# Attention denominators packed and spread by transfers, the first maxima moved into the projection

## The reference

```python
# x: (4, 1024, 128); H = 16 heads of hd = 8
xn = layernorm(layernorm(x)) * ln_g + ln_b
q, k, v = split(xn @ w_qkv + b_qkv)                       # (4, 16, 1024, 8) each
scores = einsum('bhqd,bhkd->bhqk', q, k) * hd ** -0.5
bias = (rel_pe @ w_rel)[i - j + t - 1]                    # relative position, per head
out = einsum('bhqk,bhkd->bhqd', softmax(scores + bias), v) @ w_out + b_out
x = x + layernorm(out)
# 64 experts, 8 per token, picked within 4 of 8 groups, 128 slots per expert
weights = sigmoid(layernorm(x) @ gate.T) ...              # top-k with group limits
y = sum over the 8 experts of weight * (silu(x w1) * (x w3)) w2, plus a shared expert
x = x + layernorm(y)
```

## Time and profile before

| | us |
|---|---|
| median of 3 runs (1178.47 to 1181.9) | 1181.58 |
| profiled execution | 1185.66 |
| its span, first to last instruction | 1183.8 |
| PE busy (share of the span) | 888.7 (75%) |
| DVE busy | 808.8 (68%) |
| ACT busy | 692.4 (58%) |
| POOL busy | 591.1 (50%) |
| maxima, 512 slots on DVE (mean 1.217) | 600.0 |
| reciprocal of the denominators, 8 on DVE (mean 3.344) | 26.7 |

### The profile page before, as it was taken

One profiled execution on the slowest core, in us unless ns is written; L12 is line 12 of the kernel. 1 busy time (PEld: TensorE's weight loads), 2 busy tenths in 40 slices (PEclk: granted clock), 3 DMA queues, 4 the chain that ended last, 5 costly groups with the idle time before them and its releaser, 6 DMA issues. The chain is left out here.

```text
span 1183.8 us, 16193 instructions
## 1 busy us (share of the span) xinstructions
PE 888.7 (75%) x5090; PEld 285.7 (24%) x5090; DVE 808.8 (68%) x1223; ACT 692.4 (58%) x1433; POOL 591.1 (50%) x732
## 2 busy tenths in 40 slices
PE   4647999999899999999999999999964520555400
PEld 1311222222222222222222222222212310444300
DVE  7858988889789989988988987988612310111117
ACT  4723677777687777777778767776862210322204
POOL 4720010122456455545635734654575855588847
PEclk9866999999999999999999999999996675656555
DMA  3796211133311132220002220000000010767555
GB/s 99 211 241 113 61 52 35 45 84 90 83 36 34 36 71 58 60 41 8 7 7 42 64 45 7 8 11 6 8 11 11 28 38 4 192 134 136 88 112 192
DMA packets 115499, 77.18 MB, mean 65 GB/s; under 512 B 41503, under 2 KB 99355, under 8 KB 115414
## 3 DMA queue, kind: packets, MB, share of 16 engines
q1 hardware_dynamic: 91638, 66.63, 21.5%
q0 software_dynamic: 21504, 6.79, 4.9%
q10 hardware_dynamic: 2272, 2.73, 1.3%
HBM read 38.48 MB, written 54.69 MB: 79 GB/s over the span
## 5 line engine op out<-in xcount | busy, mean ns | idle before, releaser
L737 DVE TENSOR_REDUCE half_max<-s_pair 128x2 f32<-128x1024 f32 x512 | 600.0, 1217 | 89.9 <-PE s_pair L1257 81.6
L1194 ACT ACTIVATE probs<-st_bank 128x512 f32<-128x512 f32 x1024 | 543.9, 603 | 184.7 <-PE st_bank L1270 163.8
L1057 POOL DMA_INDIRECT table<-rows,keys_i x256 | 256.6, 1003 | 178.8 <-issue 71.6
L1270 PE MATMUL st_bank<-q_stack,k_stack 98*128 98x512 bf16 (+1 forms) x1024 | 326.0, 388 | 15.4 <-issue 8.4
L1279 PE MATMUL pv_bank<-probs,values 128*16 128x512 f32 x2048 | 274.9, 608 | 4.3 <-ACT unit_out L1128 4.2
L1257 PE MATMUL s_pair<-k_stack,q_stack 64*128 64x512 bf16 x1024 | 203.5, 397 | 29.3 <-DVE half_max L737 28.2
L1257 PEld LDWEIGHTS s_pair<-k_stack,q_stack 64*128 64x128 bf16 x1024 | 48.8, 93 | 342.0 <-issue 197.9
L1270 PEld LDWEIGHTS st_bank<-q_stack,k_stack 98*128 98x128 bf16 (+1 forms) x1024 | 78.9, 97 | 177.3 <-issue 95.8
L1456 POOL DMA_INDIRECT sums<-out,ids x64 | 99.7, 1558 | 41.5 <-ACT out L1511 20.3
L1470 DVE CAST ids<-xe 128x4 uint32<-128x4 f32 x16 | 2.8, 174 | 135.4 <-DMA sums<-out,ids 83.4
L952 POOL CAST shift<-minus_max 128x16 bf16<-128x16 f32 x32 | 6.5, 202 | 117.0 <-DVE minus_max L744 116.9
(11 more groups left out here) (181 smaller groups left out, 793.9 us busy)
## 6 DMA issues: line engine op xcount, KB each, us to landing
table<-blank SPq DMA_DIRECT2D x8, 772.0 KB, 4.7
xe<-table SPq DMA_DIRECT2D x16, 386.0 KB, 5.0
q_stack<-q_image SPq DMA_DIRECT2D x96, 64.0 KB
k_stack<-k_image SPq DMA_DIRECT2D x96, 64.0 KB
s<-sums SPq DMA_DIRECT2D x24, 256.0 KB, 6.5
k_image<-k_piece SPq DMA_DIRECT2D x16, 256.0 KB, 3.1
table<-rows,keys_i POOLq DMA_INDIRECT x256
sums<-zeros SPq DMA_DIRECT2D x16, 256.0 KB
```

What stands on the lines that cost most here:

```text
L737: V.tensor_reduce(half_max[n % 2][:, h:HG:SIDE_HEADS, tile, half], s_pair[slot % S_SLOTS][:].rearrange("p (s k) -> p s k", s=SIDES), AX.X, ...
L1057: pool.indirect_dma_start(out=table, out_offset=bass.IndirectOffsetOnAxis(ap=keys_i[c % 2][:, pick:pick + 1], axis=0), in_=rows[c % 2][:, ...
L1194: A.activation(probs[:, s % P_SLOTS, :], st_bank[at % ST_BANKS][:], ACT.Exp).then_inc(bank_free, 1)
L1270: M(bank(at)[:], k_stack[g][own, tile // PER, h, tile % PER * P:(tile % PER + 1) * P], q_stack[g][own, half, h, :], start=True, stop=True) ...
```

## The change

**Values and denominators.** A head's eight value columns are followed by one column of ones (`VW` = 9) instead of eight. They are made in the projection (`vst`, two memsets on POOL instead of one on DVE) and stored and loaded with the values, as one piece per partition. `move_out` now packs the denominator row of each head into eight partitions of 64 (`packed`, 128x64), four transfers, and moves the sums by four. DVE takes the reciprocal of `packed`, and SP spreads it to `recip_t` (128x512) by eight transfers (`spread_reciprocals`), which POOL's `normalise` waits for. In SP's order this stands behind the unit's load and ahead of `put_shift(n+1)`.

**First maxima.** The 16 slots of unit 0 move to the end of the projection's block, on PE and DVE. The pair banks of the projection (psT, psQ) are now the `s_pair` banks. SP's loads back are placed one chunk later. ACT issues the bias rows of groups 1 and 2 in the attention block, SP those of group 3 behind its loads.

**Places.** The lead of 26 is reached by one more slot in 16 steps instead of 8. Reciprocal at (0, 14) for (0, 18), normalise at (0, 6) for (0, 5), y at (0, 28) for (0, 26), and the steps behind it.

**Table clears.** Two in each of units 0 to 3 instead of one in each of units 0 to 7.

```diff
+VW = HD + 1
...
-    engine.dma_start(stacks.values[:, g, :, 0, :], v_columns[:, g, b * TILES_T:(b + 1) * TILES_T]).then_inc(stacks.loaded[g], 16)
+    engine.dma_start(stacks.values[:, g].rearrange("p k c -> p (k c)"), v_columns[:, g, b * TILES_T:(b + 1) * TILES_T].rearrange("p k c -> p (k c)")).then_inc(stacks.loaded[g], 16)
...
-                if c == 1:
+                elif c == 1:
                     sp.wait_ge(bias_stored, 16 * 6)
-                if c in (1, 2):
-                    load_bias_queries(sp, stacks, bias_q_image, 0, c - 1)
-                    load_bias_keys(sp, stacks, bias_k_image, c - 1)
-                if c == 3:
+                    for side in range(SIDES):
+                        load_bias_queries(sp, stacks, bias_q_image, 0, side)
+                elif c in (2, 3):
+                    load_bias_keys(sp, stacks, bias_k_image, c - 2)
+                elif c == 4:
                     for v in range(2):
                         sp.wait_ge(q_stored[v], 16)
                         sp.wait_ge(k_stored[v], 32)
                         sp.wait_ge(v_stored[v], 16)
-                if c in (3, 4):
-                    load_side(sp, stacks, q_image, k_image, 0, 0, c - 3)
-                if c == 5:
+                if c in (4, 5):
+                    load_side(sp, stacks, q_image, k_image, 0, 0, c - 4)
+                elif c == 6:
...
-            V.memset(stacks.values[:, :, :, 1, :].rearrange("p g k c -> p (g k) c"), 1.0).then_inc(stacks.gaps_done, 1)
...
+            for slot in range(SLOTS):
+                row_max(dve, nc, stacks, slot)
...
+            for a in range(2):
+                G.memset(vst[a][:].rearrange("p g j (h c) -> p (g j h) c", h=HG)[:, :, HD:VW], 1.0).then_inc(ones_made, 1)
...
+            pe.wait_ge(xnT_done, CHUNKS)
+            pe.wait_ge(q_full_done, CHUNKS)
+            for slot in range(SLOTS):
+                row_scores(pe, nc, stacks, slot)
...
-RING_AT = {"y": (0, 26), "xf": (1, 28), "logits": (1, 31), "ranks": (3, 4)}
-NORM_Y, NORM_XF = (1, 4), (1, 22)
-RECIP, STATS_Y, STATS_X1 = (0, 18), (0, 30), (1, 14)
+RING_AT = {"y": (0, 28), "xf": (1, 28), "logits": (1, 31), "ranks": (3, 4)}
+NORM_Y, NORM_XF = (1, 5), (1, 22)
+RECIP, STATS_Y, STATS_X1 = (0, 14), (1, 0), (1, 14)
...
-NORMALISE, OUT_NORM, RESIDUAL, RES_NORM = (0, 5), (0, 7), (1, 2), (1, 5)
+NORMALISE, OUT_NORM, RESIDUAL, RES_NORM = (0, 6), (1, 0), (1, 2), (1, 5)
...
-    return 22 if n == 0 else 18
+    return (22, 20)[n] if n < 2 else 18
...
-    return min(ALL_UNITS * SLOTS, step // 2 + 1 + FIRST_LEAD + min(LEAD - FIRST_LEAD, step // 8))
+    return min(ALL_UNITS * SLOTS, step // 2 + 1 + FIRST_LEAD + min(LEAD - FIRST_LEAD, step // 16))
...
-                for h in range(HG):
-                    to = slice((HG * g + h) * HD, (HG * g + h + 1) * HD)
-                    for v, dst in enumerate((sums_t, denominators)):
-                        sp.dma_start(dst[to, :], unit_out[PART * h + v * HD:PART * h + (v + 1) * HD, :]).then_inc(unit_moved, 16)
+                    sp.wait_ge(recip_moved, SPREAD * c)
+                heads = range(HG * g, HG * (g + 1))
+                for h in heads:
+                    sp.dma_start(packed[HD * h:HD * (h + 1), :], unit_out[PART * (h % HG) + HD:PART * (h % HG) + VW, :]).then_inc(unit_moved, 16)
+                for h in heads:
+                    sp.dma_start(sums_t[HD * h:HD * (h + 1), :], unit_out[PART * (h % HG):PART * (h % HG) + HD, :]).then_inc(unit_moved, 16)
+
+            def spread_reciprocals(c):
+
+                sp.wait_ge(recip_done, c + 1)
+                if c >= 1:
+                    sp.wait_ge(normed_done, c)
+                for d in range(HD):
+                    sp.dma_start(recip_t[d:P:HD, :], packed[:]).then_inc(recip_moved, 16)
 
             load(sp, 0, 1)
...
+            for side in range(SIDES):
+                load_bias_queries(sp, stacks, bias_q_image, GROUPS - 1, side)
+                copy_bias_keys(sp, stacks, GROUPS - 1, side)
...
+                if n >= GROUPS and g == 0:
+                    spread_reciprocals(routed(n))
...
-                if n < CHUNKS:
+                if n < CHUNKS // 2:
+
                     experts = E // CHUNKS
-                    sp.dma_start(table[n * experts * CAP:(n + 1) * experts * CAP, :].rearrange("(e p) d -> p e d", p=P),
-                                 blank[:].rearrange("p (o d) -> p o d", o=1).to_broadcast([P, experts, ROW])).then_inc(blanked, 16)
-                elif n < 2 * CHUNKS:
+                    for part in (2 * n, 2 * n + 1):
+                        sp.dma_start(table[part * experts * CAP:(part + 1) * experts * CAP, :].rearrange("(e p) d -> p e d", p=P),
+                                     blank[:].rearrange("p (o d) -> p o d", o=1).to_broadcast([P, experts, ROW])).then_inc(blanked, 16)
+                elif CHUNKS <= n < 2 * CHUNKS:
                     for s in sums[1:]:
                         sp.dma_start(s[(n - CHUNKS) * CHUNK:(n - CHUNKS + 1) * CHUNK, :].rearrange("(t p) d -> p t d", p=P),
...
+            spread_reciprocals(CHUNKS - 1)
...
-                V.reciprocal(denominators[:], denominators[:]).then_inc(recip_done, 1)
+                V.reciprocal(packed[:], packed[:]).then_inc(recip_done, 1)
...
-                pool.wait_ge(recip_done, c + 1)
+                pool.wait_ge(recip_moved, SPREAD * (c + 1))
+                pool.wait_ge(unit_moved, MOVED * GROUPS * (c + 1))
                 if c >= 1:
                     pool.wait_ge(bank_ready, after(place["y", c - 1]))
-                G.tensor_tensor(att[:], sums_t[:], denominators[:], ALU.mult).then_inc(normed_done, 1)
+                G.tensor_tensor(att[:], sums_t[:], recip_t[:], ALU.mult).then_inc(normed_done, 1)
...
-            for g in range(1, GROUPS):
+            for g in (1, 2):
...
-                    mm = M(pv_bank[PART * h:PART * h + 2 * HD, :],
-                           values[:, n % GROUPS, tile].rearrange("p u c -> p (u c)")[:, h:2 * HD * HG:HG],
+                    mm = M(pv_bank[PART * h:PART * h + VW, :], values[:, n % GROUPS, tile, VW * h:VW * (h + 1)],
                            probs[:, (s + h) % P_SLOTS, :], start=(tile == 0), stop=(tile == TILES_T - 1),
```

More of the change, by code:

```diff
@@ L166, with unit_of, row_scores, row_max @@
 LOAD_BIAS = (16 * 9 * SIDES,) + (16 * 5 * SIDES,) * (GROUPS - 1)
+def unit_of(n):
+    return n // UNITS, n % UNITS // GROUPS, n % GROUPS
+def row_scores(pe, nc, stacks, slot):
+    n, i = slot // SLOTS, slot % SLOTS
+    b, half, g = unit_of(n)
+    h, tile, keys = i // 8, i // 2 % PER, i % 2
+    if i == 0 and half == 0:
+        pe.wait_ge(stacks.loaded[g], (b + 1) * LOAD)
+        pe.wait_ge(stacks.bias_rows_in[g], LOAD_BIAS[g])
+    if slot >= S_SLOTS:
+        pe.wait_ge(stacks.max_done, slot - S_SLOTS + 1)
+    for side in range(SIDES):
+        own, head = slice(MAIN_AT[side], MAIN_AT[side] + HALF_ROWS), SIDE_HEADS * side + h
+        mm = nc.tensor.matmul(stacks.s_pair[slot % S_SLOTS][:, side * CHUNK:(side + 1) * CHUNK],
+                              stacks.q[g][own, half, head, tile * P:(tile + 1) * P],
+                              stacks.k[g][own, keys, head, :], start=True, stop=True)
+    mm.then_inc(stacks.s_ready, 1)
+def row_max(dve, nc, stacks, slot, shift_done=None):
+    n, i = slot // SLOTS, slot % SLOTS
+    h, tile, half = i // 8, i // 2 % PER, i % 2
+    halves = stacks.half_max[n % 2]
+    dve.wait_ge(stacks.s_ready, slot + 1)
+    nc.vector.tensor_reduce(halves[:, h:HG:SIDE_HEADS, tile, half], stacks.s_pair[slot % S_SLOTS][:].rearrange("p (s k) -> p s k", s=SIDES),
+                            AX.X, ALU.max).then_inc(stacks.max_done, 1)
+    if i == SLOTS - 1:
+        dve.wait_ge(stacks.max_done, (n + 1) * SLOTS)
+        if n >= 1:
+            dve.wait_ge(shift_done, SHIFT_ROWS * n)
+        nc.vector.tensor_reduce(stacks.minus_max[:], halves[:].rearrange("p h t k -> p (h t) k"),
+                                AX.X, ALU.max, negate=True).then_inc(stacks.row_max_done, 1)
 def project_tokens(nc, x, ln_g, ln_b, w_qkv, b_qkv, w_rel_rows, q_table, k_table, ident_in, ident,
@@ L1244, in bank @@
                 return st_bank[at % ST_BANKS]
-            def row_scores(slot):
-                n, i = slot // SLOTS, slot % SLOTS
-                b, half, g = unit_of(n)
-                h, tile, keys_ = i // 8, i // 2 % PER, i % 2
-                if i == 0 and half == 0:
-                    pe.wait_ge(loaded[g], (b + 1) * LOAD)
-                    pe.wait_ge(bias_rows_in[g], LOAD_BIAS[g])
-                if slot >= S_SLOTS:
-                    pe.wait_ge(max_done, slot - S_SLOTS + 1)
-                for side in range(SIDES):
-                    own, head = slice(MAIN_AT[side], MAIN_AT[side] + HALF_ROWS), SIDE_HEADS * side + h
-                    mm = M(s_pair[slot % S_SLOTS][:, side * CHUNK:(side + 1) * CHUNK],
-                           q_stack[g][own, half, head, tile * P:(tile + 1) * P],
```

(2 more changed lines are left out.)

84 lines of the change are left out of this document (35 added, 49 removed).

## The result

| | before | changed |
|---|---|---|
| median of 5 | 1178.47 us (1177.8 to 1181.9) | 1191.17 us (1188.72 to 1194.04) |
| profiled execution, its span | 1185.66, 1183.8 | 1190.53, 1188.6 |
| ratio, 95% interval | | 1.0102 (1.0084 to 1.0121) |

The change costs 1%, 12 to 13 us; forecast were 1192 us for the median and +10.9 us for the profiled execution. The first profile of before is a long one of its kernel: its out copies lie 29.72 us apart in unit 8, the second one's 26.99.

What follows compares the result with a forecast made beforehand. Attention was taken as bound by PE with DVE close behind, start and tail by other chains; start +7.8, middle +0.4 and tail +2.7 summed to +10.9 us, 1196.6 profiled and 1192 median, range 1180 to 1202.

Steps and rivals of the forecast that it cites:

- Start: Attention's start: step 0 at 109.5 against 101.72, +7.8 us, as issues and loads formerly beneath the maxima come into the open.
- The hole before the boundary: End of projection: DVE idle 7.62 us before attention, so moved maxima fill at best 7.6 us.
- landing up to 1.5: Start, shift path to step 0: SP's four shift transfers land up to 1.5 us after issue; path 15.9 to 16.1.
- the path of slots 16 to 19: Start: ACT's first ten issues 5.7, landing 5.9, then 4.8 to step 0, together 16.4 us behind the boundary.
- Middle: Seven chunks routed beside attention: shorter reciprocals give -7.0 us, PE's waits for the spread and product +7.4, sum +0.4.
- bound 1.39: Middle: the most a shorter reciprocal could return per unit, PE's whole idle time for it; -9.7 us over seven.
- The stalls that I let delay PE there: Middle, unit 8: PE loses 1.14 us and about as much again, comes later, and waits only 1.0 for the product.
- the clock, which I held as a rival: Rival: longer PE waits and slower start bring more clock dips, +5 us, 1197 to 1203; with slow start, chance 0.25.
- Tail: Last chunk's uncovered chain: product +4.0 us, one scatter less before the residual -1.3, sum +2.7 (1.4 to 4.0).
- The expert and final stages, expected unchanged: Stages behind attention: the forecast expected no change in the changed profile, 0.
- Clears, 0: Table clears, two in each of units 0 to 3: POOL catches up anyway and moves have time, so 0 us.
- Faster: Rival: slot 0 at 70.0, reciprocal stalls and all three dips vanish, -7.0 us, 1175; chance 0.12.

Runs made afterwards that it cites:

- second pair: Changed kernel and kernel before, each run and profiled once more without an edit: spans 1190.0 and 1179.5 us, medians 1190.97 and 1180.75 us.
- e5: Kernel before with only the packed reciprocal, its spread and moved routing steps, sixteen columns kept: 1184.16 us, ratio 1.0036 to before.
- e6: Changed kernel with maxima back in attention, and SP issuing spread and next shift ahead of the 13 loads: 1157.47 us, ratio 0.981 to before.
- e10: e6 with table clears one in each of units 0 to 7 instead of two in units 0 to 3: 1165.22 us, ratio 0.9876 to before.
- e1: Changed kernel with the first 16 slots of maxima back in the attention block: 1177.82 us, ratio 0.9942 to before.
- e8: Changed kernel, maxima in projection with bias rows and loads of groups 1, 2 beside them, SP's order as in e6: 1159.82 us, ratio 0.9841 to before.
- e2: Changed kernel with the eight spreading transfers ahead of the 13 loads in SP's order: 1189.63 us, ratio 1.0046 to before.
- e7: Kernel before with the next unit's shift transfers ahead of the 13 loads in SP's order: 1184.53 us, ratio 1.0046 to before.
- e9: e6 with the last chunk's eight spreading transfers issued four by SP and four by ACT: 1157.01 us, ratio 0.981 to before.

## Why the prediction was right, and where its terms were off

The direction, the place of most of the cost and the waits at PE came as said. That the sum came out within 1 us of the second pair's (+10.5 against +10.9) is luck:

| us | start, to the first out copy | first to last out copy | to the load of expert rows | behind it | span |
|---|---|---|---|---|---|
| forecast | +7.8 | +0.4 | +2.7 | 0 | +10.9 |
| first pair | +9.5 | -3.5 | +1.4 | -2.6 | +4.8 |
| second pair | +11.7 | -1.4 | +3.0 | -2.8 | +10.5 |

The forecast for the second pair had the start 3.9 us too small and the rest together 4.3 too large.

- **Start: right cause, too small.** Forecast +7.8, measured +11.3 (step 0). The hole before the boundary, the boundary at 93, ACT's 11.4 us of issue came as said. The step that failed is the landing behind them: "landing up to 1.5" for the shift, from a stretch in which the DMA engines were nearly idle (share 0.08), where it was 5.6 at a share of 1.09 (the rows it was read from give 1.56); and the path of slots 16 to 19 went by ACT's first ten (11.6 to slot 16), where SP's thirteen loads ended last (14.3). That path alone puts step 0 at 112.0, the shift's landing at 113.06. I took issuing to be the cost. The Trainium skill (DMA: Bandwidth & Descriptors, Issuing engines are not separate DMA queues), which I set aside, calls the sequencer's time to issue usually small relative to the transfer. Here SP's loads took 6.4 us to issue and 7.9 more to land, so issuing was the smaller part but not small; and the copy queued behind ACT's twenty waited for nothing but their issue, 11.3 us.
- **Middle: errors that cancel.** The seven reciprocals gave more (1.68 us in units 4 and 12, forecast 1.1, bound 1.39); e5 leaves 1.52 for the packing with its moved steps. Units behind group 0's gained 0.5 each, priced at nothing. Against that stood the waits: 3.59 and 3.82, near the 3.2 forecast, and 5.54 in unit 8 where I had 1.0. The stalls that I let delay PE there didn't come (they aren't in the second profile of before either, so I had priced a chance event of one profile), and SP's loads took 1.9 us longer to issue than in unit 16 (8.1 from 313.60 to 321.68), so the spread began that much later. And each wait brought a dip to the lower clock, 3.4 or 6.8 us long: the clock, which I held as a rival, came in all three units. It cost 3.4 us net rather than 5, since before had dips too, and the larger gains hid it: -1.4 to -3.5 from the first out copy to the last, forecast +0.4.
- **Tail: right.** Product +3.7 (forecast +4.0), one scatter less before the residual, -1.3, so +2.4 there; at the load of expert rows +1.4 and +3.0. The expert and final stages, expected unchanged, were 2.6 and 2.8 us shorter; open.
- **Clears, 0:** no wait in the changed kernel answers to them, but no run had the changed kernel with eight, and the shorter last stages go with their form. As a statement on clears it is wrong: they are worth 0.66% in e6's order, 6.4 us of it in unit 8 (e10).
- **Faster:** its mechanism, the hole before the boundary, fell in e1 and e8: with every wait behind it covered, the move gains nothing. Slot 0 depends on the values of group 0, and these let it start at 73.53, when the block of e1 ends (73.55).

## What to carry to other kernels

Before work is pulled across a boundary, list what ran beneath it: here 18 us of maxima covered 20 issues and full DMA engines, and in the open these cost 14 us, for a first slot that starts 0.7 us sooner. Where one engine issues everything, as SP here, look at what stands behind its longest group: behind the 13 loads the spread was waited for (changed kernel), then the shift (e2), then the last clear (e10), until nothing urgent stood there (e6). The group to put last is the one with a unit to spare, the loads. Edits that gain nothing alone (the order in e7, the short reciprocal in e5) make up most of e6's 1.9%, and 0.66% of it hangs on the clears in four units. Two profiles of one kernel differed by 4.3 us in span here; a stall or a dip that only one of them shows isn't a term for a sum.

## What the runs showed of the hardware

- In these stretches the landing went by the DMA share around a transfer more than by its size: the shift's four transfers (2 KB each) landed at most 1.6 us behind their issue at a share of 0.08 and 5.6 at 1.09; group 1's values (144 KB) reached PE 2.3 us after the start of their issue at 0.37 and 8.4 at 1.10.
- Each of PE's waits of 3.5 us or more in units 8, 16 and 24, in all runs, came with 3.4 to 6.8 us at the lower clock, and in e2 so did one of 3.02. Shorter ones did at times: before, PE waits 1.19 us in all seven units with a reciprocal, and three of them have a dip of 3.4 us in one profile and four in the other. In e6, without such waits, the mean over 282 us is 1.00.
- The reciprocal goes by columns: 3.34 us at 128x512, 1.743 at 128x256, 0.553 at 128x64.
- A spreading transfer from SBUF to SBUF of 32 KB holds SP's queue for 0.64 us (eight in 5.11); four on ACT in e9 took 2.82, 0.71 each.
